# Attention weighing with two-part values: one 128-column product per key block in place of two of 64 columns

## The reference

```python
def _gat_layer(h, mask, b):
    scores = einsum('...nd,...md->...nm', h, h)
    scores = where(mask, scores, NEG)
    attn = softmax(scores, axis=-1)
    return einsum('...nm,...md->...nd', attn, h) + b
h = einsum('bnc,hdc->bhnd', x, Wh)
out_h = _gat_layer(h, mask[None, None], bh[None, :, None, :])   # 8 batches x 4 heads
z = leaky_relu(cat(out_h), 0.2)
h2 = einsum('bnk,dk->bnd', z, Wo)
z2 = leaky_relu(_gat_layer(h2, mask[None], bo), 0.2)            # 8 batches
out = layernorm(z2) * gamma + beta
```

## Time and profile before

| | |
|---|---|
| Median of 3 runs | 3122.71 us (3119.36 to 3128.4) |
| Profiled execution, its own time | 3127.07 us |
| Its span, first to last instruction | 3125.3 us |
| TensorE products busy | 2923.1 us (94%), 49770 |
| TensorE weight loads busy | 2168.0 us (69%), 49770 |
| VectorE busy | 2681.5 us (86%), 5523 |
| ACT busy | 2275.4 us (73%), 2654 |
| GpSimd busy | 2587.7 us (83%), 1458 |

### The profile page before, as it was taken

The page is one execution under the profiler, slowest core; times in us unless marked ns, Lnnn a source line. Parts: engine busy times, 40 slices in busy tenths (PEclk is TensorE's granted clock), DMA queues, the critical chain, the costliest instruction groups (busy, mean ns, idle before and its releaser), DMA issues. The chain is left out here.

```text
span 3125.3 us, 124905 instructions
## 1 busy us (share of the span) xinstructions
PE 2923.1 (94%) x49770; PEld 2168.0 (69%) x49770; DVE 2681.5 (86%) x5523; ACT 2275.4 (73%) x2654; POOL 2587.7 (83%) x1458
## 2 busy tenths in 40 slices
PE   7957999999999999999999999999998889999990
PEld 5435777777777777777777777777776867777760
DVE  6966888888888888988889888988897579999988
ACT  1267777777777777777777777777776567777773
POOL 4465999998898999999999989999999079888882
PEclk8979999999999999999999999999999999999995
DMA  6139899889999889998899898898987878898773
GB/s 245 48 132 342 146 167 165 157 155 161 159 166 163 157 158 168 165 165 158 157 171 165 166 150 160 164 164 168 160 158 144 294 152 158 163 165 163 155 140 89
DMA packets 1443985, 514.30 MB, mean 165 GB/s; under 512 B 1359503, under 2 KB 1417293, under 8 KB 1441357
## 3 DMA queue, kind: packets, MB, share of 16 engines
q1 hardware_dynamic: 1443532, 507.36, 82.7%
HBM read 105.30 MB, written 66.06 MB: 55 GB/s over the span
## 5 line engine op out<-in xcount | busy, mean ns | idle before, releaser
L583 POOL TENSOR_TENSOR low<-probs 128x1024 f16<-128x1024 f32 x1280 | 2395.7, 1893 | 358.3 <-ACT probs L870 255.0
L870 ACT ACTIVATE probs<-scores,shifted_max 128x2048 f32<-128x2048 f32 x640 | 1282.5, 2004 | 223.6 <-DVE shifted_max L1077 219.9
L736 PE MATMUL ps<-operands 128*128 128x512 f16 x2560 | 973.7, 380 | 7.9 <-DMA v_parts<-h_d 5.8
L737 PE MATMUL ps<-operands 128*128 128x512 f16 x2560 | 972.2, 380 | 0.0
L1072 DVE CUSTOM_DVE_ANT_0 scores<-ps,mask,neg_max 128x1024 f32<-128x1024 f32 x640 | 821.6, 1284 | 126.4 <-issue 73.3
L898 ACT COPY probsT<-ps 128x1024 bf16<-128x1024 bf16 x640 | 647.6, 1012 | 374.7 <-PE ps L745 374.7
L745 PEld LDWEIGHTS ps<-ident,probs 128*128 128x128 bf16 x10240 | 650.1, 98 | 370.0 <-issue 202.3
L1072 DVE CUSTOM_DVE_ANT_0 scores<-ps,mask 128x1024 f32<-128x1024 f32 x640 | 781.3, 1221 | 134.1 <-PE ps L737 124.0
L745 PE MATMUL ps<-ident,probs 128*128 128x128 bf16 x10240 | 780.5, 219 | 9.9 <-DVE probsT L1086 6.9
L756 PE MATMUL ps<-v_parts,probsT 128*128 128x64 f16 x10240 | 685.4, 193 | 5.5 <-issue 5.5
L755 PE MATMUL ps<-v_parts,probsT 128*128 128x64 f16 x10240 | 685.0, 193 | 1.4 <-DVE outs L1136 1.4
(11 more groups left out here) (156 smaller groups left out, 1734.7 us busy)
## 6 DMA issues: line engine op xcount, KB each, us to landing
operands<-hT_d SPq DMA_DIRECT2D x40, 512.0 KB, 4.3
operands<-hT_d SPq DMA_DIRECT2D x80, 256.0 KB, 4.0
v_parts<-h_d SPq DMA_DIRECT2D x40, 512.0 KB, 4.9
probsT<-low SPq DMA_TRANSPOSE x1280, 3.5
z_d<-outs SPq DMA_DIRECT2D x38, 512.0 KB, 3.9
h_d<-probs SPq DMA_DIRECT2D x32, 512.0 KB, 5.9
hT_d<-probsT SPq DMA_DIRECT2D x32, 512.0 KB, 5.3
scores<-z_d SPq DMA_DIRECT2D x32, 512.0 KB, 4.9
```

What stands on the lines that cost most here:

```text
L583: pool.tensor_tensor(low[:, u, w], probs[:, u, w], high[:, u, w], ALU.subtract).then_inc(sem(f"low{half}"), 1)
L736: pe.matmul(ps[:, b, :], hi_lo[:, p, t * P:(t + 1) * P], hi_lo[:, p, w], start=True, stop=False)
L737: scored = pe.matmul(ps[:, b, :], hi_lo[:, p, t * P:(t + 1) * P], lo_hi[:, p, w], start=False, stop=True)
L870: act.activation(probs[:, 1 - u, :], scores[:, 1 - u, :], ACT.Exp, bias=shifted_max[:, 1 - u:2 - u], scale=-1.0, accum_out=row_sum[:, held ...
```

## The change

L755 and L756 become one product per key block with both value parts as its 128 moving columns, into a slot of 128 PSUM columns per tile (`out_slots`); a group fills its bank of 512 columns. The first 64 columns of a slot hold upper probabilities by upper values, to which L728 adds the lower probabilities as before; the second 64 hold upper probabilities by lower values. VectorE then runs the four bias instructions on the first halves, waits on a semaphore for its own last one, and runs four more that multiply the second halves by the same reciprocals and add what the first four wrote. Also, 112 transposes of the identity stand ahead of layer 1 in place of 32.

```diff
-        def out_slot(tt):
-
-            return ps[:, 6 + tt // 4 % 2, tt % 4 * D:(tt % 4 + 1) * D]
+        def out_slots(tt):
+
+            return ps[:, 6 + tt // 4 % 2, tt % 4 * P:(tt % 4 + 1) * P]
+
+        def out_slot(tt, part=0):
+
+            return out_slots(tt)[:, part * D:(part + 1) * D]
...
-            for _ in range(32):
+            for _ in range(112):
                 pe.transpose(banks16(0, 1)[:, 0:P], ident_h[:, :], ident_h[:, :])
...
                         w = highT[:, 1 - u, c * P:(c + 1) * P]
-                        pe.matmul(out_slot(tt), w, v_parts[:, held, c * P:c * P + D], start=(c == 0), stop=False)
-                        added = pe.matmul(out_slot(tt), w, v_parts[:, held, c * P + D:(c + 1) * P], start=False, stop=False)
+                        added = pe.matmul(out_slots(tt), w, v_parts[:, held, c * P:(c + 1) * P], start=(c == 0), stop=False)
...
+                    def biased(tt):
+                        return outs[:, held, tt * D:(tt + 1) * D] if second else group_tmp(k)[:, tt % 4 * D:(tt % 4 + 1) * D]
+
                     for tt in range(4 * k, 4 * k + 4):
-                        added = dve.scalar_tensor_tensor(outs[:, held, tt * D:(tt + 1) * D] if second else group_tmp(k)[:, tt % 4 * D:(tt % 4 + 1) * D], out_slot(tt), row_inv[:, held, tt:tt + 1],
-                                                         rows[:, 1, :] if second else bias[:, old, :] if isinstance(old, int) else bias[:, bass.ds(old, 1), :].rearrange("p o d -> p (o d)"),
-                                                         ALU.mult, ALU.add)
+                        first_half = dve.scalar_tensor_tensor(biased(tt), out_slot(tt), row_inv[:, held, tt:tt + 1],
+                                                              rows[:, 1, :] if second else bias[:, old, :] if isinstance(old, int) else bias[:, bass.ds(old, 1), :].rearrange("p o d -> p (o d)"),
+                                                              ALU.mult, ALU.add)
+                    first_half.then_inc(sem("first_halves"), 1)
+                    dve.wait_ge(sem("first_halves"), old * 4 + k + 1)
+                    gate(dve, "dve")
+                    for tt in range(4 * k, 4 * k + 4):
+                        added = dve.scalar_tensor_tensor(biased(tt), out_slot(tt, 1), row_inv[:, held, tt:tt + 1], biased(tt), ALU.mult, ALU.add)
                     added.then_inc(sem("n_biased" if second else "out_biased"), 1)
```

## The result

The changed kernel takes 3253.94 us (median of 4 runs, 3250.99 to 3256.55) against 3125.56 us of the kernel before (4 runs, 3119.36 to 3136.68): ratio 1.0408, 95% interval 1.0389 to 1.0426, 128 us slower. The forecast was 3275, within a range from 3222 to 3312.

The account below looks back on a forecast made before the run. TensorE's own issue (4.02 of 4.10 us a tile) nearly bounds layer 1, VectorE layer 2. Layer 1 122 + layer 2 33 + start 2.5 - relief 5 = + 152.5 on the median 3122.71 gives 3275 us, range 3222 to 3312.

Parts of the forecast that it names:

- The link: Layer 1: VectorE's lateness behind the bias instructions delays its copy, stalling TensorE's next transposes 1 to 1, about 1.22 us a group.
- Rival 2: The copy isn't the link, only VectorE's sum counts: layer 1 + 4, layer 2 + 19 us, 3148 in all; chance 0.05.
- Rival 3: Faster: VectorE's 1.01 us is hidden before the next score products and TensorE's gain counts, 3101 us; chance 0.04.
- rival 4: TensorE's stalls of 1.2 us make the granted clock drop in places, + 128 us more, 3400; chance 0.03.
- The group: Four tile steps in layer 1: from 16.24 to 17.18 us, + 0.95 each, + 122 us over 128 groups.
- the second set: Four more VectorE bias instructions a group: 0.76 us plus 0.25 for the wait between sets, 1.01 together.
- The product's saving: TensorE: 16 products of 128 columns replace 32 of 64, a gain of 0.037 us a tile, 0.15 a group.
- For layer 2: VectorE hardly waits there, so the added time joins the same chain: 32 x 1.02 = + 33 us, at least + 19.
- the relief: TensorE's lower-half products wait less for DMA because transfers get 6% more time: - 5 us, bounds - 25 and 0.
- The start: 80 more transposes on TensorE ahead of layer 1, 4.5 us, passed on as about 2.5; bounds 0 and 4.5.
- The upper end of the range: 3312 us: the added VectorE time at 1.2 us a group, + 29, and no relief.

Follow-up runs that it names:

- kernel 2: Kernel before plus only the second set of four bias instructions, rereading the same 64 columns, with two 64-column products and 32 transposes: 3265.64 us, ratio 1.0456.
- kernel 5: Changed kernel with only VectorE's copy of turned half 0 moved between its two masks: 3122.42 us, ratio 1.0008 to the kernel before.
- kernels 9 and 10: Kernel before and changed kernel, each with VectorE's copy between its masks and L728 moved between the score halves: 3075.3 and 3059.76 us.
- Kernels 7 and 8: Kernel before and changed kernel, each with operand loads cut to 128 columns in all but a layer's first two instances: 3112.03 and 3255.12 us.
- kernel 4: Changed kernel with 32 transposes ahead of layer 1 in place of 112: 3254.79 us against 3253.94.
- kernel 1: Changed kernel's 128-column products alone, without the second set of bias instructions and with 32 transposes: 3127.22 us, ratio 1.0008 to the kernel before.
- kernel 3: Changed kernel with the second set writing to its own buffer, so without the wait for the first set: 3215.95 us, ratio 1.0298 to the kernel before.
- 6: Kernel before with only VectorE's copy moved between its two masks: 3100.14 us, ratio 0.9920 to the kernel before.

## Why the prediction was right

**The link.** The prediction put all of the slowing on VectorE's copy, just in time in every step and late behind the bias instructions. The after profile has the copy's end 0.15 us before the transposes, as before, kernel 2 has the slowing without the products, and kernel 5 takes away all but 22 us of it by moving the copy alone. Rival 2 (VectorE's sum counts) is out in layer 1, where VectorE still had 0.85 us a group to spare; in layer 2 the copy's place and VectorE's sum would both give about 1.01 a group, and no run parts them. Rival 3 (all of it absorbed) is out. So is rival 4: the clock stayed at 1.00 in the middle of layer 1. In layer 2 it was 0.93 from 2600 to 2700 us, where the layer starts (its first shifted maximum is at 2616.2 us, after TensorE had stood 8.41 us for the load of `v_parts`), and 1.00 from 2700 to 3000. The two traces show layer 1 99.1 us longer and layer 2 27.6 us, from the first to the last shifted maximum.

**The group.** Foretold 17.18 a group in layer 1, measured 17.20; the 1.01 us of the second set are 1.00 between the starts of the sets, which with 0.78 behind it make 1.02 more than one set's 0.76. The product's saving, foretold as 0.037 us a tile, is (17.28 - 17.20)/4 = 0.02 between kernel 2 and the changed one, and (16.10 - 15.92)/4 = 0.045 where nothing hides it (kernels 9 and 10); the 16 products, 1.06 us in all, start (1.06 - 0.22)/15 = 0.056 apart. For layer 2 the prediction read a group of 16.82 us; the median of the layer is 16.47, but only the added part went into the sum.

**What was mis-sized.** The added time, + 152.5 in the sum, was 24 us too high, and the term that failed is the relief. I took - 5 from the waits of one line in 1000 us in the middle of layer 1, 3.8 us. That was a calm part: over the layer, from 320 to 2400 us, the same trace has

```profile
PE ps L728 <- DMA probsT<-low: 12.6, 22, 1.9
```

Measured: in layer 1 the mean lay 0.19 above the median before and 0.04 after, 128 x 0.15 = - 19; in layer 2 0.20 and 0.09, 32 x 0.11 = - 4. Kernels 7 and 8 show that the operand loads make some 10 us of it. Two things can bring the relief: the transfers land in time, as in the changed kernel's trace (0.8 us of waits in layer 1), or they are late in a step in which TensorE would stand still for the copy anyway, as in kernel 4's. The start was taken at 2.5 us; kernel 4 shows no difference that its runs can tell, and why the 4.5 us don't count is open, as said there. The sum then is 0.93 x 128 + 1.02 x 32 - 19 - 4 = 119 + 33 - 23 = 129, and 128 was measured. The bound of - 25 for the relief held, with little to spare. The upper end of the range, 3312, is 3 us above what the terms named with it give (3275 + 29 + 5).

## What to carry to other kernels

When an in-order engine does several things a step, look for the one that ends only just ahead of its user in every step; in layer 1 here, whatever was added before it was paid whole, although the engine had 0.85 us of idle time left in each group. First try another order: here moving one copy was worth about 130 us to the changed kernel and 22 to the old one, and a second move turned what was left of the loss into a gain of 15.5 us. Compare a change within each order, since the order decides its worth. Price a change by the median of the rhythm and look at the mean apart from it, over the whole layer and not a calm part of it: here waits for late transfers gave 23 us back when the period grew, and took some when it shrank (kernel 1).

## What the runs showed of the hardware that was not expected

- A short vector instruction that waits for the one ahead of it and reads its result starts 0.24 us later than one that follows at once (1.00 against 0.76 between the first starts of two sets of four, the changed kernel and kernel 3).
- The granted clock stayed at 1.00 in the middle of layer 1 of the changed kernel although TensorE stood still for about 1.05 us in each 17.2, but it was 0.83 from 310 to 330 us at the ragged start of layer 1 in kernel 4. Of the kernel before, one group of layer 1 was 4.0 us too long: TensorE waited 1.89 us for a DMA transpose, 0.46 us having gone before it, and the granted clock was 0.57 in the 4 us that followed. The next score products start 0.41 us apart, at the lower of the clock's levels, 1.2 GHz, in place of 0.22. So 2.35 us of waits for late transfers cost 4.0 us. The three products, and the stretch from 1848 to 1852 us:

```profile
1848.52 0.61 PE L728 MATMUL ps<-v_parts,probsT 128*128 128x64 f16 x8 [1.89 <-DMA probsT<-low]
1848.94 0.61 PE L736 MATMUL ps<-operands 128*128 128x512 f16 x1
1849.35 0.63 PE L737 MATMUL ps<-operands 128*128 128x512 f16 x1
```

```profile
1848.00:1852.00 4.00, 3.48 (x23) 2.12 (x24) 0.94 (x1) 0.72 (x3) 3.60 (x3) 0.57 0.77 172
```

- Idle time of the transposes' weight loads was put under "issue" in the kernel before (74.9 us in 227 waits), and still is after (138.8 us; the 61.4 us named on the products are in part the same stops). In kernels 5, 6, 9 and 10, whose copy is early, this row is absent between 1000 and 2000 us: it was the wait for VectorE's copy, in nearly every step. The name of a releaser is a hint, the times are the evidence.
